# Two layers of attention on one core: the first layer's maximum pass with its PSUM banks filled otherwise

## The reference

```python
a1 = _attn(q, k1, v1, causal=True)     # latent keys, 512
a2 = _attn(q, ks, vs, causal=False)    # the 64 selected rows as keys
a3 = _attn(q, kw, vw, causal=True)     # window keys, 512
out = g[:, 0] * a1 + g[:, 1] * a2 + g[:, 2] * a3
```

## Time and profile before

| | us |
|---|---|
| median of the timed runs (3) | 3108.49 |
| lowest and highest | 3104.93, 3109.99 |
| the profiled execution: its own time | 3114.26 |
| its span in the profile | 3112.4 |

### The profile page before, as it was taken

The page is one execution under the profiler, slowest core; times in us unless marked ns, Lnnn a source line. Parts: engine busy times, 40 slices in busy tenths (PEclk is TensorE's granted clock), DMA queues, the critical chain, the costliest instruction groups (busy, mean ns, idle before and its releaser), DMA issues. The chain is left out here.

```text
span 3112.4 us, 54041 instructions
## 1 busy us (share of the span) xinstructions
PE 2896.0 (93%) x18640; PEld 2071.5 (67%) x18640; DVE 1963.0 (63%) x6274; ACT 1477.5 (47%) x3132; POOL 962.9 (31%) x1700
## 2 busy tenths in 40 slices
PE   4999899989999899999999999999999989999877
PEld 3676676666766677666776667766677666766654
DVE  3666656665676656766567666577566676565644
ACT  1445344464445544455444563445544464445443
POOL 0233233332334223333133332333223332323331
PEclk7999999999999999999999999999999999999989
DMA  3011001100110001100101001110011000110000
GB/s 112 29 37 30 27 25 32 31 14 21 45 32 24 24 32 31 32 19 24 37 26 39 17 25 30 39 31 12 29 39 32 25 16 25 32 32 17 14 8 29
DMA packets 58703, 91.47 MB, mean 29 GB/s; under 512 B 19904, under 2 KB 32704, under 8 KB 58176
## 3 DMA queue, kind: packets, MB, share of 16 engines
q1 hardware_dynamic: 58432, 88.01, 9.7%
HBM read 81.68 MB, written 5.24 MB: 28 GB/s over the span
## 5 line engine op out<-in xcount | busy, mean ns | idle before, releaser
L1822 ACT ACTIVATE PR<-work 128x512 f32<-128x512 f32 (+1 forms) x1088 | 639.5, 598 | 723.6 <-PE work L1148 620.0
L1430 DVE CUSTOM_DVE_ANT_0 work<-work,KEEPB 128x128 f32<-128x128 f32 (+3 forms) x1536 | 665.7, 477 | 87.0 <-PE work L1109 85.1
L1945 POOL TENSOR_SCALAR_AFFINE_SELECT PR<-PR 128x256 f32<-128x256 f32 (+1 forms) x960 | 356.9, 376 | 886.9 <-ACT PR L1822 882.9
L1109 PE MATMUL work<-BIG 96*128 96x448 f32 (+8 forms) x1664 | 453.1, 364 | 24.8 <-DVE NMX L1430 14.5
L1146 PE MATMUL work<-BIG 99*128 99x512 f32 (+4 forms) x1152 | 420.4, 365 | 14.1 <-DVE BIG L1411 5.6
L1934 POOL TENSOR_TENSOR TOK<-AB 128x256 f32<-128x256 f32 (+1 forms) x320 | 219.9, 688 | 631.6 <-DVE AB L1392 592.0
L1182 PE MATMUL outs<-PR,ONES 128*32 128x512 f32 (+4 forms) x2304 | 404.8, 458 | 0.0
L1411 DVE TENSOR_TENSOR BIG<-work,BIG 96x512 fp32r<-96x512 f32 (+1 forms) x320 | 191.6, 604 | 321.4 <-ACT BIG L1710 321.2
L1147 PE MATMUL work<-BIG 96*128 96x512 f32 (+4 forms) x1152 | 382.9, 332 | 0.0
L1148 PE MATMUL work<-BIG 96*128 96x512 f32 (+4 forms) x1152 | 381.1, 331 | 0.0
L1109 PEld LDWEIGHTS work<-BIG 96*128 96x128 f32 (+1 forms) x1664 | 278.7, 199 | 149.0 <-issue 61.9
(11 more groups left out here) (170 smaller groups left out, 4627.2 us busy)
## 6 DMA issues: line engine op xcount, KB each, us to landing
NRM<-park SPq DMA_DIRECT2D x112, 192.0 KB, 3.1
WKW<-w_kw_dram SPq DMA_DIRECT2D x64, 256.0 KB, 2.7
WSEL<-w_sel_dram SPq DMA_DIRECT2D x64, 256.0 KB, 3.0
R<-park SPq DMA_DIRECT2D x72, 64.0 KB, 2.0
HN<-x_dram SPq DMA_DIRECT2D x8, 512.0 KB, 5.1
X<-x_dram SPq DMA_DIRECT2D x8, 512.0 KB, 4.1
out_dram<-X SPq DMA_DIRECT2D x7, 512.0 KB, 3.3
R<-park SPq DMA_DIRECT2D x16, 192.0 KB, 3.2
```

The costliest lines, as they stand in the source:

```text
L1109: last = mm(ps[:, col:col + n], q, k, start=(i_mm == 0), stop=(i_mm == len(u["mm"]) - 1))
L1430: last = v.tensor_tensor_reduce(ps[:, lo:hi], ps[:, lo:hi], KEEPB[:, T - (hi - lo):T], -1.0, -NEG, ALU.add, ALU.min, dst)
L1822: a.activation(PR[0:rows, j % NP, :], ps[0:rows, :], ACT.Exp).then_inc(exp_ready, 1)
L1945: gp.affine_select(blocks, blocks, [[0, len(cols)], [1, P]], ALU.is_ge, 0.0, base=0, channel_multiplier=-1).then_inc(exp_masked, 1)
```

## The change

Four of a head's six banks get other contents, and one bank is shared by the two heads. A head has five banks: for the latent keys one of 512 columns (query tile 3) and one of 384 + 128 (tiles 2 and 0), the same for the window keys, and one of 256 + 256 (tile 1 of both). All these segments end in a diagonal block and are taken with the masked operation. The selected keys of both heads and all four query tiles, 8 x 64 columns, are in one bank made by eight matmuls; one plain reduction with eight results takes their maxima. It is the sixth of the pair's now eleven banks. NPART, the joining operation and `max_ready` go; the transposes of the maxima wait until the last bank has been read. The due times in AFTER, TAIL, PRO, MID_A, MID_B, MID_C, HEADS and PROJ are other numbers, most by some tenths of a unit.

```diff
 def max_units0():
     out = []
     for h in range(2):
-        out += [
-            dict(mm=[(h, "k1", 0, 448, 0, 3)], mask=[], segs=[(0, 64, A2, h, 3), (64, 448, A1, h, 3)]),
-
-            dict(mm=[(h, "k1", 448, 128, 0, 3), (h, "kw", 0, 384, 128, 2)], mask=[0, 384],
-                 segs=[(0, 128, None, h, 3), (128, 512, A3, h, 2)]),
-            dict(mm=[(h, "kw", 0, 512, 0, 3)], mask=[384], segs=[(0, 512, A3, h, 3)]),
-            dict(mm=[(h, "k1", 0, 448, 0, 2)], mask=[320], segs=[(0, 64, A2, h, 2), (64, 448, A1, h, 2)]),
-            dict(mm=[(h, "k1", 0, 320, 0, 1), (h, "kw", 0, 128, 320, 0)], mask=[192, 320],
-                 segs=[(0, 64, A2, h, 1), (64, 320, A1, h, 1), (320, 448, A3, h, 0)]),
-            dict(mm=[(h, "k1", 0, 192, 0, 0), (h, "kw", 0, 256, 192, 1)], mask=[64, 320],
-                 segs=[(0, 64, A2, h, 0), (64, 192, A1, h, 0), (192, 448, A3, h, 1)]),
-        ]
+        for a, src, k0 in ((A1, "k1", KEEP), (A3, "kw", 0)):
+            out += [dict(mm=[(h, src, k0, 512, 0, 3)], mask=[384], segs=[(0, 512, a, h, 3)]),
+                    dict(mm=[(h, src, k0, 384, 0, 2), (h, src, k0, 128, 384, 0)], mask=[256, 384],
+                         segs=[(0, 384, a, h, 2), (384, 512, a, h, 0)])]
+        out.append(dict(mm=[(h, "k1", KEEP, 256, 0, 1), (h, "kw", 0, 256, 256, 1)], mask=[128, 384],
+                        segs=[(0, 256, A1, h, 1), (256, 512, A3, h, 1)]))
+    out.insert(5, dict(mm=[(h, "k1", 0, KEEP, KEEP * (NT * h + t), t) for h in range(2) for t in range(NT)], mask=[],
+                       segs=[]))
     return out
...
-AFTER = [dict(pv=2.67, recip=1.97, scale=3.42, late_recip=2.37, late_scale=5.46, scale_gap=0.91, last_recip=1.73, last_scale=3.91, piece=-2.58, gap=0.66, piece_tr=1.99, max=4.98, max_gap=0.31, mt=1.97, rows=-5.38, kr=0.44, val=3.0),
-         dict(odd=3.2, pv=3.12, recip=2.71, scale=5.16, last_recip=2.0, last_scale=4.22, max=-0.18, max_gap=1.03, mt=2.45, piece=32.73, gap=1.08, piece_tr=1.44, kr=37.93, val=-0.0)]
+AFTER = [dict(pv=2.67, recip=1.97, scale=3.44, late_recip=3.46, late_scale=4.11, scale_gap=0.9, last_recip=1.82, last_scale=3.62, piece=-2.58, gap=0.66, piece_tr=1.99, max=5.62, max_gap=0.31, mt=1.97, rows=-5.38, kr=0.46, val=3.51),
+         dict(odd=3.2, pv=3.12, recip=2.98, scale=4.71, last_recip=2.07, last_scale=4.22, max=-0.18, max_gap=1.03, mt=2.45, piece=32.73, gap=1.08, piece_tr=1.71, kr=37.27, val=-0.18)]
...
             def transpose_maxima(s, layer, p):
                 if layer == 0:
-                    pe.wait_ge(max_ready, NPAIR * s + p + 1)
+                    was_read(pe, work, work_read, (s, 0, "max", p, len(MAX_UNITS[0]) - 1))
                     for h in range(2):
...
+                if not u["segs"]:
+
+                    last = v.tensor_reduce(NMX[:, p % 2, 16:24], ps[:, :].rearrange("p (c k) -> p c k", k=KEEP), AX.X,
+                                           ALU.max, negate=True)
                 for n, (lo, hi, att, h, qt) in enumerate(u["segs"]):
-                    if att is None:
-                        dst = NPART[:, h:h + 1]
-                    else:
-                        c = (att * 2 + h) * NT + qt
-                        dst = NMX[:, p % 2, c:c + 1]
+                    c = (att * 2 + h) * NT + qt
+                    dst = NMX[:, p % 2, c:c + 1]
...
                 read_work(last, (s, layer, "max", p, i))
-                if layer == 0 and i == len(MAX_UNITS[0]) - 1:
-
-                    was_read(dve, work, work_read, (s, layer, "max", p, i))
-                    c = NT - 1
-                    dst = NMX[:, p % 2, c:c + NT + 1:NT]
-                    v.tensor_tensor(dst, dst, NPART[:, :], ALU.min).then_inc(max_ready, 1)
```

More of the change, by code:

```diff
@@ L200, in tail_steps @@
     return [x + (t,) for x, t in zip(names, at)]
[L203 to L208, removed]
+TAIL = [[("wo_early", 4.75), ("wo_last", 5.37), ("tail_add", 0, 5.37), ("tail_add", 1, 6.02),
+         ("tail_var", 0, 6.19), ("tail_var", 1, 8.04), ("tail_ln", 0, 8.24), ("tail_ln", 1, 9.61),
+         ("hT", 3, 0, 9.76), ("hT", 3, 1, 9.88), ("sign", 0, 11.47), ("sign", 1, 12.24)],
+        [("wo_early", 6.05), ("wo_last", 6.77), ("tail_add", 0, 6.87), ("tail_add", 1, 7.08),
+         ("tail_var", 0, 8.79), ("tail_var", 1, 10.47), ("tail_ln", 0, 10.85), ("tail_ln", 1, 11.01),
+         ("hT", 3, 0, 11.93), ("hT", 3, 1, 12.02), ("sign", 0, 12.16), ("sign", 1, 13.78)]]
 TAIL_ORDER = [x[0:-1] for x in tail_steps(range(12))]
 PRO = [("pro", 0, 58.95), ("pro", 1, 63.32), ("pro_pe", 0, 74.53), ("pro_act", 2, 75.05), ("pro_pe", 1, 76.51),
[L215 to L218, removed]
+       ("pro_act", 3, 76.67), ("pro", 3, 77.45), ("pro_pe", 6, 78.31), ("pro_act", 4, 78.85),
+       ("pro_pe", 2, 80.63), ("pro", 4, 81.58), ("pro_pe", 3, 84.34), ("pro_act", 5, 85.48), ("pro", 5, 86.02),
+       ("pro_act", 6, 87.59), ("pro", 6, 87.83), ("pro", 7, 89.05), ("pro", 8, 89.14), ("pro", 9, 89.6),
+       ("pro_pe", 4, 93.35), ("pro", 10, 94.14), ("pro_pe", 5, 96.19), ("pro", 11, 96.95), ("pro", 12, 102.87)]
 def first_half(ln, hT, fc):
@@ L235, in second_half @@
         + [("qk", t, at) for t, at in enumerate(qk)]
-MID_A = [[("ln", 1, 0, 8.17), ("ln", 1, 1, 9.2), ("hT", 1, 0, 9.72), ("hT", 1, 1, 10.6), ("fc", 0, 0, 11.42),
[3 rows of a table removed]
-MID_B = [("y", 0, 0, 8.85), ("y", 0, 1, 9.75), ("y", 0, 2, 11.26), ("y", 0, 3, 12.5), ("spike", 0, 0, 19.73),
-         ("spike", 0, 1, 20.16), ("spike", 0, 2, 20.42), ("spike", 0, 3, 21.23), ("spike", 0, 4, 22.07),
-         ("spike", 0, 5, 22.58), ("var", 2, 0, 22.62), ("y", 1, 0, 36.11), ("y", 1, 1, 37.47), ("y", 1, 2, 40.06),
+MID_A = [[("ln", 1, 0, 8.17), ("ln", 1, 1, 9.2), ("hT", 1, 0, 9.72), ("hT", 1, 1, 10.09), ("fc", 0, 0, 11.42),
[3 rows of a table added]
@@ L247 @@
+MID_B = [("y", 0, 0, 8.85), ("y", 0, 1, 9.75), ("y", 0, 2, 11.26), ("y", 0, 3, 12.92), ("spike", 0, 0, 20.1),
+         ("spike", 0, 1, 20.16), ("spike", 0, 2, 20.29), ("spike", 0, 3, 21.1), ("spike", 0, 4, 22.07),
+         ("spike", 0, 5, 22.58), ("var", 2, 0, 22.62), ("y", 1, 0, 34.16), ("y", 1, 1, 37.47), ("y", 1, 2, 40.12),
          ("y", 1, 3, 40.63), ("spike", 1, 0, 44.18), ("spike", 1, 1, 45.5), ("spike", 1, 2, 46.17),
-         ("spike", 1, 3, 46.23), ("spike", 1, 4, 46.8), ("spike", 1, 5, 46.86), ("var", 2, 1, 47.27),
@@ L249 @@
-         ("fc", 1, 0, 21.88), ("fc", 1, 1, 23.52), ("fc", 1, 2, 29.56), ("fc", 1, 3, 33.91), ("ln", 2, 0, 49.71),
-         ("ln", 2, 1, 51.46), ("hT", 2, 0, 52.56), ("hT", 2, 1, 53.64), ("qk", 0, 54.66), ("qk", 1, 58.8),
-         ("qk", 2, 59.48), ("qk", 3, 63.65)]
+         ("spike", 1, 3, 46.44), ("spike", 1, 4, 46.8), ("spike", 1, 5, 46.86), ("var", 2, 1, 47.27),
+         ("fc", 1, 0, 21.76), ("fc", 1, 1, 23.5), ("fc", 1, 2, 29.56), ("fc", 1, 3, 33.91), ("ln", 2, 0, 49.71),
+         ("ln", 2, 1, 51.46), ("hT", 2, 0, 52.56), ("hT", 2, 1, 53.06), ("qk", 0, 54.6), ("qk", 1, 58.86),
@@ L254 @@
+         ("qk", 2, 59.42), ("qk", 3, 63.59)]
 MID_C = [("ln", 1, 0, -3.6), ("ln", 1, 1, -3.0), ("hT", 1, 0, -2.2), ("hT", 1, 1, -1.6), ("fc", 0, 0, 0.5),
[L255 to L258, removed]
@@ L259 @@
-         ("spike", 1, 1, 24.06), ("spike", 1, 2, 24.36), ("spike", 1, 3, 24.39), ("spike", 1, 4, 24.96),
[3 rows of a table removed]
[L265 to L270, removed]
@@ L273 @@
[L273 to L276, removed]
+         ("fc", 0, 1, 2.2), ("fc", 0, 2, 4.12), ("fc", 0, 3, 6.06), ("y", 0, 0, 8.46), ("y", 0, 1, 8.88),
+         ("y", 0, 2, 9.6), ("y", 0, 3, 10.4), ("spike", 0, 0, 11.5), ("spike", 0, 1, 11.64),
@@ new lines @@
+         ("spike", 0, 2, 11.94), ("spike", 0, 3, 12.24), ("spike", 0, 4, 12.7), ("spike", 0, 5, 12.7),
+         ("var", 2, 0, 14.54), ("y", 1, 0, 20.0), ("y", 1, 1, 21.38), ("y", 1, 2, 21.6), ("y", 1, 3, 22.4),
+         ("spike", 1, 0, 23.76), ("spike", 1, 1, 24.06), ("spike", 1, 2, 24.36), ("spike", 1, 3, 24.39),
+         ("spike", 1, 4, 24.77), ("spike", 1, 5, 25.26), ("var", 2, 1, 25.3), ("fc", 1, 0, 12.36),
+         ("fc", 1, 1, 14.2), ("fc", 1, 2, 15.9), ("fc", 1, 3, 17.74), ("ln", 2, 0, 26.0), ("ln", 2, 1, 26.7),
@@ new lines @@
+         ("hT", 2, 0, 28.0), ("hT", 2, 1, 28.6), ("qk", 0, 29.79), ("qk", 1, 31.7), ("qk", 2, 33.64),
+         ("qk", 3, 34.76)]
+HEADS = [[("clear", 0, 95.15), ("clear", 1, 99.26), ("stack", 0, 95.91), ("stack", 1, 99.35), ("heads", 0, 100.13),
+          ("heads", 1, 101.9), ("stack", 2, 100.64), ("heads", 2, 103.48), ("stack", 3, 103.26),
+          ("heads", 3, 106.17), ("v", 0, 103.54), ("v", 1, 122.55)],
+         [("clear", 0, -18.75), ("clear", 1, -17.76), ("stack", 0, -18.18), ("stack", 1, -16.49),
+          ("heads", 0, -16.47), ("heads", 1, -16.16), ("stack", 2, -15.23), ("heads", 2, -13.57),
+          ("stack", 3, -14.9), ("heads", 3, -12.09), ("v", 0, -14.64), ("v", 1, -14.49)]]
@@ L279, in attention_steps @@
+PROJ = [[("proj_early", 6.01), ("proj_last", 7.17), ("proj_add", 0, 7.97), ("proj_add", 1, 8.33),
+        ("var", 1, 0, 8.5), ("var", 1, 1, 8.61)],
```

(4 more changed lines are left out.)

## The result

The changed kernel takes 3155.56 us (median of 4 runs, 3147.99 to 3160.22) against 3106.71 before: a ratio of 1.0155, 95% interval 1.0136 to 1.0174, so 48 us more (42 to 54). That is slower, as forecast, inside the stated range of 3100 to 3158 and close to its upper end; the forecast itself was +26. The profiled execution lies at the fast end: its span is 3146.2 us, 33.8 more than before. So the two profiles show some 34 of the 48 us: by the pages 21.9 us more in which TensorE is busy and 11.9 more in which it stands still.

A forecast was written before the change was run, and what follows sets the result against it. TensorE was taken to bound the kernel, busy 261.1 of 265.8 us in a first-layer pass. +38 us for matmuls, -12 for shorter waits on VectorE and zero for due times gave +26: 3134 us, stated range 3100 to 3158.

The forecast's parts named there:

- the price of a short matmul: On TensorE, in the first layer's score products: each 64-column matmul of the shared bank was taken to cost 0.11 us.
- rivals 2: Shared bank's weight loads hide, 0.06 us a matmul and below; the kernel gets faster, low end 3093 us; chance 0.10.
- 3 (0.19): Shared bank's short matmuls each pay a full-length load of 0.19 us, +69 us in sum, 3177 us; chance 0.08.
- the "few" that was named: TensorE's idle time behind the first layer's maxima was to fall from 13.0 us to a few.
- The other due times: In both layers, the remaining due times shift by tenths of a unit; no sign in the rows, so zero us.
- the transposes' move: First layer's transposes of the maxima move from 10.36 to 10.69; their work fits the time left, so nothing.
- The price: TensorE's extra time in the first layer for the new matmuls: +0.60 us a pair, +38 us over 64 pairs.
- the relief: TensorE waits less for VectorE's maxima in the first layer: between nothing and 38 us, taken as 12 us.
- rival 1: In the first layer, 38 us of TensorE's waits go and cancel the +38 of the matmuls: 3108 us; chance 0.12.
- Rival 4: Re-fitted due times halve TensorE's waits for second-layer maxima (27.8 us) and stacks (25.1): 3108 us or below; chance 0.10.

## Why the prediction was right or wrong

**What held.** The sign, the range, and the price of a short matmul. The eight start 0.11 us apart, as the forecast took from the earlier trace rows, so rivals 2 (0.06 and below) and 3 (0.19) are out. The maximum with eight results takes 0.690 us against 0.68 worked out from the earlier trace rows. TensorE's idle time ahead of score products behind the maxima falls from 13.0 to 3.2 us (1.6 + 1.3 + 0.3 in the rows by form), which is the "few" that was named. Both sums leave rows out: with the score products of 320 and 192 columns it was 14.9 us, and with the units of 384 columns it is 3.9.

**The step that failed** is one term of the sum: *"The other due times shift by tenths of a unit in both layers, without a sign that rows could give; zero"*, and with it the transposes' move, *"so nothing"*. They held only that the work fits the time, not that the order stays. Two runs split the 48 us, each against the kernel before:

| step | ratio | us on 3107 | step alone |
|---|---|---|---|
| the changed banks, order of before kept (transposes at 10.36) | 1.0014 (1.0005 to 1.0024) | +4 | +4 |
| with the other new due times as well (maxima at 4.98) | 1.0115 (1.0098 to 1.0132) | +36 | +31 |
| with the maxima at 5.62, the changed kernel | 1.0155 (1.0136 to 1.0174) | +48 | +12 |

So +26 was forecast for what costs about 4, and 0 for what costs 43 or so. The steps of 31 and 12 us are good to some 6 and 8 us, and hold in this order of steps. The forecast was near the result by luck: it was too dear in one term and too cheap in the other, and the mechanism that it gave for the loss is not the main one. The profiles say the same. From the run with the order kept to the changed kernel, TensorE's busy time grows by 6.4 us and its standing still by 30.3:

```profile
PE 2911.5 (94%) x19024; PEld 2104.7 (68%) x19024; DVE 1925.1 (62%) x5634; ACT 1479.5 (48%) x3132; POOL 974.4 (31%) x1700
```

That page is of the run with the order kept; its span is 3109.5 us.

**The price and the relief.** With the order kept, the first layer's pass shown (266.7 us) has 2.9 us more of TensorE's work than that of before and 2.0 us less standing still. Over the whole run, by the pages, TensorE is busy for 15.5 us more and stands still for 18.4 less, where the forecast had +38 and -12. So the price was too large by this measure and the relief too small; how 0.60 us a pair by the starts becomes 15.5 us of busy time isn't shown, and a load that comes late under a running matmul, in the kernel before too, counts as busy. From one pair's maxima to the next pair's, the 56 distances inside the eight passes sum to 1972.4 us before (the joining operation's starts), 1962.6 with the order kept and 2004.2 in the changed kernel (the starts of the maximum with eight results). Inside the passes the new banks are thus some 10 us ahead in these single executions; between the passes, where the same starts are 792.1 us apart in all before and 801.3 then, they lose 9. In the timed runs the new banks cost 4 us (2 to 7). So the new work and the waits that are gone nearly cancel: rival 1, given 0.12, is what the banks do by themselves, with smaller terms than its 38 and 38 by busy time. The runs with wide matmuls point the same way from the other side. Eight short matmuls are 0.88 us, two of 256 columns 2 x 0.12: 0.64 us a pair, 41 us in all. Measured were 17 us (twelve banks) and 22 (the changed kernel), and in the second TensorE's loads wait for VectorE twice as long as with the short ones, 56.5 us for 27.5.

**VectorE.** 115 us were to be saved, 45 were. The sum was made from durations, and those of VectorE don't add up either: in the run with eight maxima, 512 of 213 ns are 109 us and take 72.8. The forecast held that TensorE covers nearly all of it; a longer list still reaches the end by about half (12 of 22 us, some 8 on either side, the run with eight maxima).

**The pass of the first layer** was to grow by 3.3 us with TensorE as busy as now. The one shown grew by 7.2; by the distances above, 31.8 us over 56 pairs, it is 4.5 us for eight pairs. Of the 7.2, 2.6 are standing still, the sign of the order and not of the loads. The second layer's pass stayed as it was, as forecast.

**Rival 4** has the wrong sign. The due times of the change cost rather than pay. They are a mend all the same: the changed banks with the old table as it stands stand at 1.0196, 13 us above the new one's 1.0155, because there the transposes of the maxima, due at a sum over the count of banks, had slipped ahead of the next pair's second piece. The forecast worked out 10.36 and 10.69 and asked whether the work still fits the time left. It didn't ask which steps change places, and that was the question: 0.31 of a unit decided over 57 us.

**What stays open.** How the 31 us divide among the other new due times. A sign is in the waits: pieces and units stand behind ScalarE's copies for 16.4 and 8.9 us, where the run with the order kept shows 0.8 and none. At 10.69 the copies of the maxima, due 0.4 later at 11.09, come behind the exponentials of the pair's last unit (due 11) in ScalarE's list, and at 10.36 (10.76) ahead of them. The timeline of the changed kernel shows it (L1812 are the exponentials):

```profile
1304.19 0.59 ACT L1812 ACTIVATE PR<-work 64x512 f32<-64x512 f32 x1 [2.13 <-PE work L1143]
1304.80 1.06 ACT L1700 ACTIVATE BIG<-work 3x512 fp32r<-3x512 f32 x2
1305.43 0.30 PEld L1042 LDWEIGHTS work<-WQ,NQT 96*128 96x128 f32 x2 [1.26 <-ACT BIG L1700]
```

All 20 of these waits (13 + 7) end with such a copy, with a unit's exponentials just ahead of it. That these 25 us of late loads make most of the 31 isn't shown: as TensorE's idle time they are 11.3 us (5.6 + 5.7, ahead of the same pieces and units; 0.43 us in the case shown, where the load waited 1.26), and no run put the transposes of the changed kernel at 10.36 or the other tables back one by one. The 12 us of the later maxima have no sign of their own there, as these waits are the same in both runs.

## What to carry to other kernels

Where due times set the order and one of them is a sum over a count of steps, a change of that count moves other steps: write out for each engine, before and after, which step passes which, since one place cost 57 us here and the new layout itself about 4. A short matmul with weights of its own took 0.11 us here, at 64 columns as at 128, but take off the waits that it covers before calling that a loss: here 0.64 us a pair was read from the starts, and about half of it was measured. And when a layout comes with a new schedule, time the layout in the old order first, with every moved step put back by hand; the old table as it stands is not that order.

## What the runs showed of the hardware

- A score product of 64 columns with its own weights starts 0.11 us after the one ahead of it, at a granted clock of 1.00, and two of three products of 128 columns in a row do the same. So the columns don't set this pace; that the load does is the likely reading, which no run tried by itself. The Trainium skill ("TensorE: Matmul & The Clock Gate", Back-to-back issue gap) has about 25 ns for 64 columns taken alone; with a load for each, this trace shows four times that.
- Eight results cost a plain maximum nothing to speak of: 0.690 us over 512 columns, where 384 columns with one result take 0.545 and 1.03 ns a column more would give an estimated 0.68.
- Short operations of VectorE in a row hide much of their length in one another: eight maxima of 64 columns in a row last 0.213 us each and take 0.142 each of its busy time (72.8 / 512).
